# Two warm-up runs of TensorE resized and the gathers of the second block spread differently over its first two tiles

## The chip, the cores and the metric

The kernel runs on one core of a Trainium2 chip. The metric is the device time of one execution in microseconds, the median of several. Its engines are named as in the profile: PE (TensorE matmul), PEld (TensorE weight load), DVE (VectorE), ACT (ScalarE), POOL (GpSimd), SP (SyncE).

## The reference

The kernel is a recommendation tower. For each of 1024 samples, 39 ids pick one row of 16 numbers each out of 39 tables; then three layers of compressed interaction are applied, and a small three-layer network ends it:

```python
e = jnp.stack([tbl_0[ids[:, 0]], ..., tbl_38[ids[:, 38]]], axis=1)     # 1024 x 39 x 16
x0 = xk = e
for idx, (W, b) in enumerate([(w0, b0), (w1, b1), (w2, b2)]):          # each 128 units
    z = jax.nn.relu(jnp.einsum('bhd,bkd,hks->bsd', x0, xk, W) + b[None, :, None])
    # layers 0 and 1: the first 64 units are the next xk, the other 64 go out; layer 2: all 128 go out
logit = jnp.sum(jnp.concatenate(direct, axis=1), axis=-1)              # 1024 x 256
h = jnp.maximum(jnp.concatenate([logit, dense_ctx], axis=1) @ W_top1 + b_top1, 0.0)
h = jnp.maximum(h @ W_top2 + b_top2, 0.0)
y = h @ W_top3
```

All is in float32. 26 tables have 1000 to 125000 rows and are gathered by indirect DMAs; 13 small ones are gathered like the others, except in the first block.

## The kernel before

**Tiles.** The 1024 samples are 8 blocks of 128. A block's 16 embedding columns are cut into 4 tiles of 4 columns, so a tile is 512 wide (4 columns by 128 samples) and there are 32 tiles. Every engine has its own program and walks over steps -2 to 31; step t does layers 1 and 2 of tile t, layer 0 of tile t+1, and the transposes of tile t+2. Steps -2 and -1 are the start, where layers 1 and 2 are absent.

**A product.** DVE multiplies the layer's input with replicated rows of the embedding (`x_rep`, loaded from DRAM by SP and ACT queues for each tile) into 128x1024 products, ten pairs per layer 1 or 2, four for layer 0. `KINDS` (line 33) says how each pair goes on. "U" goes to PE as it is. For "P" and "V" ACT makes a rounded head of the product (line 701) and POOL ("P", line 583) or DVE ("V", line 904) the rest, product minus head, and PE multiplies heads and rests (line 1040). A P pair therefore passes DVE, ACT, POOL and PE in turn. Layer 1 is "UPVPUPVPVP" (P at pairs 1, 3, 5, 7, 9), layer 2 is "UUVUPUVPVP" (P at pairs 4, 7, 9).

**Gathers.** One block's ids need 39 indirect DMAs of 128 rows each (`gather`, line 566), all issued by POOL between its rests. They land in `gathered`, in order of fields, in four groups of 12, 12, 8 and 7 with a semaphore each. ACT's `spread` (line 713) waits for all four groups and copies `gathered` to `emb` (line 719), from which PE transposes tiles; after the copy `gathered` is free and POOL may take the next block's ids (`copy_indices`, line 562). The first block is gathered at the start: 26 big tables by DMA, 13 small ones by one-hot matmuls on PE (lines 1003 to 1008, called the sums below).

The second block's 39 gathers are dealt out by line 41: `GATHERS_EARLY[0]` of them before step 0 (lines 611 to 613), `GATHERS_EARLY[1]` in step 0 and `GATHERS_EARLY[2]` in step 1 (lines 621 to 623). Inside a step `rests` places them by line 40:

```python
GATHERS_AFTER = {1: (0, 1, 0, 0, 8), 2: (2, 2, 2)}   # after the n-th P rest of layer 1, of layer 2
...
                while layer == 2 and fields:
                    gather(fields.pop(0))             # what is left, after the last rest
```

So nine fields fit into layer 1 of a step (one after pair 3, eight after pair 9); what is beyond goes into layer 2, two after pair 4, two after pair 7, the rest after pair 9. The `spread` of the second block is in ACT's step 1, after the head of layer 2's last pair and ahead of all heads of step 2 (lines 783 and 784). Later blocks use 10, 10, 11 and 8 fields in their four steps (line 42), and are not touched.

**PE's start.** PE spreads the ids of the small tables (line 986), transposes the dense features (line 990), waits for the one-hots, runs `keep_busy(FIRST_WARM_UP)`, waits for the last table terms (line 1002), does the sums, waits for the small rows and for the first three groups of gathers, runs `keep_busy(WARM_UP)`, waits for the weights of layer 0, and transposes the first two tiles (line 1094):

```python
            def keep_busy(count):
                for n in range(count):
                    nc.tensor.matmul(z[1][:], onehots[:, n % 4, :],
                                     onehots[:, 0:N // P, :].rearrange("p c b -> p (c b)"), start=True, stop=True)
```

Nothing reads what these matmuls (line 997, bf16, 512 columns) write. After the transposes come ACT's copies (lines 731, 767), SP's store of the rows (lines 536, 539), the first loads of `x_rep` by SP and ACT (lines 519, 688), layer 0 of tile 0 (lines 1017, 1074), and step 0.

Of the kernel before, what the change touches and what calls it, by code (L numbers as in the profile page):

```python
# [37 lines left out]
WHOLE_SLOTS = 6  # L38
SPLIT_SLOTS = 4
GATHERS_AFTER = {1: (0, 1, 0, 0, 8), 2: (2, 2, 2)}  # L40
GATHERS_EARLY = (20, 10, 9)
GATHERS_OF_TILE = (10, 10, 11, 8)
D2_AFTER = 6
XT_AFTER = 3
# [8 lines left out]
EMB_AFTER = 6  # L53
D0_AFTER = 4
AHEAD = 2
WARM_UP = 34
SMALL_RUNS = ((0, 3), (17, 22), (26, 31))
SMALL = tuple(f for start, stop in SMALL_RUNS for f in range(start, stop))
TABLE_ROWS = 125
TERMS = 3  # L60
IDS_PER_BANK = 4
FIRST_WARM_UP = 12
TABLES_OF_ACT = 4
FILL_UP = 10
GATHER_GROUPS = (12, 12, 8, 7)
# [33 lines left out]
def build_kernel(nc, dense_ctx, ids, tables, W_top1, b_top1, W_top2, b_top2, W_top3,  # L99
# [19 lines left out]
    with ExitStack() as ctx:  # L119
# [262 lines left out]
        def wait_gathers(eng, t, groups):  # L382

            for g in groups:
                first = GATHER_GROUPS[g] - sum(group_of[f] == g for f in SMALL)
                eng.wait_ge(s_gather[g], t.blocks(16 * GATHER_GROUPS[g], 16 * first))
# [174 lines left out]
        def _(pool):  # L561
# [4 lines left out]
            def gather(f):  # L566

                nc.gpsimd.indirect_dma_start(  # L568
                    gathered[:, f, :], None, tables[f],
                    bass.IndirectOffsetOnAxis(ap=idx[:, f:f + 1], axis=0)).then_inc(s_gather[group_of[f]], 16)  # L570
# [40 lines left out]
            early = list(range(FIELDS))  # L611
            for f in early[:GATHERS_EARLY[0]]:
                gather(f)
            del early[:GATHERS_EARLY[0]]
            def body(t):
                if not has_layers12(t):
                    return
                ahead = t.plus(AHEAD)
                k = ahead.first % TPB
                refill = None  # L620
                if t.turn is None and t.first < LOOP0:
                    fields = early[:GATHERS_EARLY[1 + t.first]]
                    del early[:GATHERS_EARLY[1 + t.first]]
                elif t.turn is None and ahead.blocks(1, 1) >= BLOCKS:
                    fields = []
                else:
                    first = sum(GATHERS_OF_TILE[:k])
                    fields = list(range(first, first + GATHERS_OF_TILE[k]))
                    if k == 0:
                        refill = ahead.blocks(1, 1)  # L630
                rests(t, 1, fields, refill)
                rests(t, 2, fields)
# [349 lines left out]
        def _(pe):  # L982
# [11 lines left out]
# [6 lines that stand above are left out]
            pe.wait_ge(s_onehot, len(SMALL))  # L1000
            keep_busy(FIRST_WARM_UP)
            pe.wait_ge(s_low, 1)
# [7 lines left out]
            wait_gathers(pe, Tile(0), range(3))  # L1010
            keep_busy(WARM_UP)
            pe.wait_ge(s_w0, 1)
# [143 lines left out]
```

## Time and profile before

| | us |
|---|---|
| median of 3 runs (lowest, highest) | 1265.41 (1264.4, 1268.2) |
| the profiled execution, its own time | 1277.38 |
| its span, first to last instruction | 1275.6 |
| PE busy (share of the span) | 1234.2 (97%) |
| DVE busy | 1162.4 (91%) |
| POOL busy | 901.5 (71%) |
| ACT busy | 708.0 (56%) |

The span is the table's second time less 1.8 us that lie around it. The profiled execution took 12.0 us more than the median of the runs without a profile. A busy PE is counted from the start of a matmul to its modelled end, so 97% says that there are few gaps, not that the array works at its peak.

### The profile page before, as it was taken

Reading aid. Unit: us, or ns where it says so; the run is one execution under the profiler, and the core shown is the slowest. Engines: PE = TensorE matmul, PEld = TensorE weight load, DVE = VectorE, ACT = ScalarE, POOL = GpSimd, SP = SyncE. Lnnn points to the kernel's source line nnn. Section 1 sums busy time; section 2 is a strip of 40 time slices with the busy share of each in tenths; the row PEclk is TensorE's granted clock in tenths of the full one; section 3 lists DMA queues with packets and bytes.
Section 4 is the critical chain, followed back from the end, with each engine's and each line's share of the span. In section 5 each row is a group of like instructions: output and inputs, shape, how many; then the busy total and the mean of one; then the engine's idle time right before and its main releaser. Section 6 shows DMA issues by size and latency. Waiting matters only on the chain.

```text
span 1275.6 us, 15546 instructions
## 1 busy us (share of the span) xinstructions
PE 1234.2 (97%) x4268; PEld 785.7 (62%) x4268; DVE 1162.4 (91%) x1045; ACT 708.0 (56%) x741; POOL 901.5 (71%) x569
## 2 busy tenths in 40 slices
PE   3779999999999999999999999999999999999999
PEld 2446666666666666666666666666666666666654
DVE  7359999999999999999999999999999999999990
ACT  1236655456655665566655655557555655655542
POOL 7568777776887788787877778786878755555440
PEclk7789999999999999999999999999999999999999
DMA  7299887778988888889888888889888878898500
GB/s 212 60 227 214 188 184 183 193 197 208 223 181 183 189 195 198 197 202 220 203 179 188 191 195 200 201 209 221 180 185 187 197 194 198 198 218 198 132 23 0
DMA packets 135922, 234.42 MB, mean 184 GB/s; under 512 B 16403, under 2 KB 25101, under 8 KB 135787
## 3 DMA queue, kind: packets, MB, share of 16 engines
q1 hardware_dynamic: 84335, 151.67, 51.7%
q10 hardware_dynamic: 41994, 79.99, 24.5%
q0 software_dynamic: 9568, 2.47, 2.0%
q8 instruction: 10, 0.16, 0.1%
q14 instruction: 15, 0.12, 0.0%
HBM read 230.21 MB, written 6.23 MB: 185 GB/s over the span
## 4 chain that ended last, share of the span: by engine, by line
PE 80%; DVE 9%; DMA 4%; issue 4%; another core or an unknown queue 1%; ACT 1%; POOL 0%; ACTq 0%; DVEq 0%; SPq 0%
PE z_odd L1040 32%; PE z_even L1040 30%; PE z_odd L1074 6%; PE z_even L1074 6%; DMA x_rep<-x_rows 4%; DVE whole L871 4%; DVE whole_psum L871 1%; DVE x_rep L811 1%; PE whole_psum L1068 1%; DVE rest L904 1%; PE x_even L1068 1%; PE x_odd L1068 1%; PE x_even L1094 1%; PE x_odd L1094 1%
## 5 line engine op out<-in xcount | busy, mean ns | idle before, releaser
L583 POOL TENSOR_TENSOR rest<-whole,head 128x1024 fp32r<-128x1024 f32 x256 | 611.2, 2398 | 251.4 <-ACT head L701 237.5
L871 DVE TENSOR_TENSOR whole<-x_banks,x_rep 128x1024 f32<-128x1024 f32 x448 | 534.7, 1218 | 40.0 <-ACT x_banks L659 36.8
L701 ACT CAST head<-whole 128x1024 fp32r<-128x1024 f32 x256 | 268.7, 1050 | 155.4 <-DVE whole L871 107.7
L568 POOL DMA_INDIRECT gathered<-in_tbl,idx x299 | 287.6, 962 | 82.2 <-issue 74.6
L701 ACT CAST head<-whole_psum 128x1024 fp32r<-128x1024 f32 x192 | 194.8, 1014 | 137.5 <-DVE whole_psum L871 125.2
L871 DVE TENSOR_TENSOR whole_psum<-x_banks,x_rep 128x1024 f32<-128x1024 f32 x192 | 235.8, 1228 | 6.1 <-DMA x_rep<-x_rows 3.3
L904 DVE TENSOR_TENSOR rest<-whole_psum,head 128x1024 fp32r<-128x1024 f32 x192 | 234.7, 1222 | 0.5 <-ACT head L701 0.5
L1040 PE MATMUL z_odd<-head,w_rest 128*128 128x512 f32 x427 | 196.9, 461 | 1.5 <-POOL rest L583 0.9
L1040 PE MATMUL z_odd<-whole,w_whole 128*128 128x512 f32 x400 | 186.8, 596 | 3.7 <-DVE whole L871 3.7
L1040 PE MATMUL z_even<-head,w_rest 128*128 128x512 f32 x405 | 186.4, 460 | 0.8 <-POOL rest L583 0.7
L1040 PE MATMUL z_odd<-head,w_head 128*128 128x512 f32 x460 | 181.9, 395 | 0.0
L1040 PE MATMUL z_even<-head,w_head 128*128 128x512 f32 x436 | 172.4, 395 | 0.0
L1040 PE MATMUL z_even<-whole,w_whole 128*128 128x512 f32 x368 | 170.5, 592 | 0.0
L1040 PE MATMUL z_odd<-rest,w_head 128*128 128x512 f32 x427 | 168.7, 395 | 0.0
L1040 PE MATMUL z_even<-rest,w_head 128*128 128x512 f32 x405 | 160.0, 395 | 0.0
L1040 PEld LDWEIGHTS z_odd<-whole,w_whole 128*128 128x128 f32 x400 | 76.2, 191 | 74.9 <-issue 64.5
L1074 PE MATMUL z_even<-whole,w0s 117*128 117x512 f32 x238 | 106.8, 598 | 3.9 <-DVE whole L871 3.9
L1040 PEld LDWEIGHTS z_even<-whole,w_whole 128*128 128x128 f32 x368 | 69.7, 189 | 64.0 <-issue 58.2
L1040 PEld LDWEIGHTS z_odd<-head,w_head 128*128 128x128 f32 x460 | 86.6, 188 | 32.2 <-issue 15.2
L1040 PEld LDWEIGHTS z_odd<-head,w_rest 128*128 128x128 f32 x427 | 80.5, 189 | 36.5 <-issue 14.9
L1040 PEld LDWEIGHTS z_even<-head,w_head 128*128 128x128 f32 x436 | 82.1, 188 | 30.6 <-issue 14.4
L1040 PEld LDWEIGHTS z_even<-head,w_rest 128*128 128x128 f32 x405 | 76.5, 189 | 31.8 <-issue 14.1
(117 smaller groups left out, 1007.8 us busy)
## 6 DMA issues: line engine op xcount, KB each, us to landing
x_rep<-x_rows ACTq DMA_DIRECT2D x128, 512.0 KB, 11.6
x_rep<-x_rows SPq DMA_DIRECT2D x128, 512.0 KB, 12.2
x_shift<-x_rows SPq DMA_DIRECT2D x93, 546.0 KB
x_rep<-x_rows ACTq DMA_DIRECT2D x32, 384.0 KB
x_rep<-x_rows SPq DMA_DIRECT2D x32, 384.0 KB
x_rep<-x_rows SPq DMA_DIRECT2D x32, 256.0 KB
gathered<-in_tbl,idx POOLq DMA_INDIRECT x299
x_rows<-xt_and_ctx SPq DMA_DIRECT2D x32, 78.0 KB
```

Source lines behind the costliest of these rows:

```text
L568: nc.gpsimd.indirect_dma_start(gathered[:, f, :], None, tables[f], bass.IndirectOffsetOnAxis(ap=idx[:, f:f + 1], axis=0)).then_inc(s_gathe ...
L583: nc.gpsimd.tensor_tensor(rest[:, split_slot(product)], whole_slot(product), head[:, split_slot(product)].bitcast(F32), ALU.subtract).then ...
L701: nc.scalar.copy(head[:, split_slot(product)], src).then_inc(s_head, 1)
L811: nc.vector.tensor_tensor(onehots[:, before_small[i]:before_small[i + 1], :], ids_bank[i].unsqueeze(1).to_broadcast([TABLE_ROWS, each, P]) ...
L871: nc.vector.tensor_tensor(out[0:rows, 0:width, :], xk[0:rows, :].unsqueeze(1).to_broadcast([rows, width, N]), x0, ALU.mult).then_inc(s_pro ...
L904: nc.vector.tensor_tensor(rest[:, split_slot(product)], whole_psum[:], head[:, split_slot(product)].bitcast(F32), ALU.subtract).then_inc(s ...
L1040: mm = nc.tensor.matmul(zz[:], w, x, start=(j == PE_ORDER[layer][0] and i == 0), stop=(j == PE_ORDER[layer][-1] and i == len(terms) - 1))
L1068: mm = nc.tensor.matmul(out, w, x, start=(i == 0), stop=(i == len(terms) - 1))
L1074: mm = nc.tensor.matmul(z_of(t, 0)[:], w0s[0:ROWS0, i, :], whole_slot((t, 0, j))[0:ROWS0, i - 2 * j, :], start=(i == 0), stop=(i == CHUNKS ...
L1094: mm = nc.tensor.transpose(out[0:ROWS0, i * P:(i + 1) * P], rows, ident[:])
```

## The change

Three constants change: the second run of warm-up matmuls has 10 instead of 34, the first 24 instead of 12, and the 39 gathers of the second block are dealt out as 12, 14 and 13 instead of 20, 10 and 9.

```diff
-GATHERS_EARLY = (20, 10, 9)
+GATHERS_EARLY = (12, 14, 13)
...
-WARM_UP = 34
+WARM_UP = 10
...
-FIRST_WARM_UP = 12
+FIRST_WARM_UP = 24
```

## Rows read from the trace of the kernel before

**Rows 1.** The chain of waits in order of time: start us, us, what.
```profile
390.80 6.01 PE z_even L1074 x14
...
426.96 6.01 PE z_odd L1074 x14
```

**Rows 2.** Timeline of PE, the start: start us, us, engine, line, operation, [idle before <-releaser].
```profile
22.09 4.42 PE L997 MATMUL z_odd<-x_rep 125*128 125x512 bf16 x12
31.23 1.14 PE L1005 MATMUL z_even<-x_rep 125*128 125x48 bf16 x24 [4.71 <-DVE x_rep L828]
...
40.58 2.56 PE L1005 MATMUL z_even<-x_rep 125*128 125x48 bf16 x60 [1.18 <-issue]
...
44.58 8.16 PE L997 MATMUL z_odd<-x_rep 125*128 125x512 bf16 x34 [0.40 <-DVE gathered L838]
52.58 0.88 PE L1094 MATMUL x_even<-ident,emb 128*117 128x128 f32 x4
```

**Rows 3.** Timeline of ACT, the start.
```profile
38.51 1.54 ACT L655 CAST w_head<-whole 128x256 fp32r<-128x256 f32 x3
44.63 1.75 ACT L719 COPY emb<-gathered 128x1872 f32<-128x1872 f32 x1 [4.59 <-DVE gathered L838]
```

**Rows 4.** Stretches: length, busy us of five engines, granted clock, DMA share, GB/s.
```profile
29.00:45.80 16.80, 7.18 (x119) 5.56 (x120) 5.45 (x12) 5.34 (x11) 7.40 (x7) 0.50 0.31 69
46.00:52.60 6.60, 6.60 (x33) 3.07 (x31) 4.31 (x8) 0.39 (x1) 5.06 (x4) 1.00 0.03 4
```

**Rows 5.** Timeline of POOL, ahead of step 0 and in step 0.
```profile
72.67 0.94 POOL L568 DMA_INDIRECT gathered<-in_tbl,idx  x1 [0.30 <-issue]
82.61 4.73 POOL L583 TENSOR_TENSOR rest<-whole,head 128x1024 fp32r<-128x1024 f32 x2 [9.00 <-ACT head L701]
...
106.46 2.40 POOL L583 TENSOR_TENSOR rest<-whole,head 128x1024 fp32r<-128x1024 f32 x1
109.02 0.96 POOL L568 DMA_INDIRECT gathered<-in_tbl,idx  x1 [0.16 <-issue]
...
114.48 2.42 POOL L583 TENSOR_TENSOR rest<-whole,head 128x1024 fp32r<-128x1024 f32 x1 [1.18 <-ACT head L701]
```

**Rows 6.** Timeline of PE: last pair of step 0, first P pair of step 2.
```profile
117.81 0.39 PE L1040 MATMUL z_odd<-head,w_rest 128*128 128x512 f32 x1
...
157.47 0.48 PE L1040 MATMUL z_odd<-head,w_rest 128*128 128x512 f32 x1
```

**Rows 7.** Timeline of POOL, step 1.
```profile
141.42 0.94 POOL L568 DMA_INDIRECT gathered<-in_tbl,idx  x1 [0.30 <-issue]
142.55 2.39 POOL L583 TENSOR_TENSOR rest<-whole,head 128x1024 fp32r<-128x1024 f32 x1 [0.18 <-issue]
147.07 2.38 POOL L583 TENSOR_TENSOR rest<-whole,head 128x1024 fp32r<-128x1024 f32 x1 [2.14 <-ACT head L701]
```

**Rows 8.** Timeline of ACT, end of step 1 and first head of step 2.
```profile
150.47 1.75 ACT L719 COPY emb<-gathered 128x1872 f32<-128x1872 f32 x1
153.05 1.05 ACT L701 CAST head<-whole 128x1024 fp32r<-128x1024 f32 x1 [0.82 <-DVE whole L871]
```

**Rows 9.** Queue of the gathers, packets in 37.2-39.5, 146-148, 186-192 us: packets, MB, share.
```profile
q0 software_dynamic: 64, 0.02, 7.7%
...
q0 software_dynamic: 26, 0.01, 2.8%
...
q0 software_dynamic: 64, 0.02, 2.1%
```

**Rows 10.** Timeline of POOL: the gathers beside those packets.
```profile
37.29 0.94 POOL L568 DMA_INDIRECT gathered<-in_tbl,idx  x1 [0.30 <-issue]
...
181.32 0.96 POOL L568 DMA_INDIRECT gathered<-in_tbl,idx  x1
182.59 0.94 POOL L568 DMA_INDIRECT gathered<-in_tbl,idx  x1 [0.30 <-issue]
```

**Rows 11.** Waits of DVE, 190 to 310 us: us in total, times, longest.
```profile
DVE whole L871 <- DMA x_rep<-x_rows: 2.8, 2, 1.8
```

## The prediction, made before the changed kernel ran

> **What bounds the kernel now.** I read the chain of waits first. From about 85 us to the end it is nearly all PE, and in the steady part a step takes 426.96 - 390.80 = 36.16 us [rows 1], with hardly a gap in PE. Nothing that the change touches runs there: it touches only what lies before step 2. So whatever is gained or lost before about 170 us is carried to the end one to one, and two stages have to be priced. The timeline of PE at the start shows the first. The sums run until 44.2, the second warm-up run starts at 44.58, has 34 matmuls in 8.16 us, and the first transpose follows at 52.58 with no idle time noted before it [rows 2]. The transposes need `emb`, whose copy ended at 44.63 + 1.75 = 46.4 [rows 3]. So here the warm-up itself is what the transposes wait for, and with them the stores, the loads of `x_rep` and step 0. The other stage is the hand-over to the second block's gathers in steps 0 and 1: POOL's timeline [rows 5, 7], when PE is due for what POOL makes [rows 6], and ACT's copy of the second block [rows 8].
>
> **The change, part by part.**
>
> *First warm-up, 12 to 24.* The 12 took 4.42 us from 22.09 and ended at 26.5; the sums began only at 31.23, after 4.71 us idle [rows 2]. Twelve more at the same mean of 0.37 us end at 30.9. They fit: cost nothing, covered by DVE's table terms with 0.3 us to spare. If the clock were high all the way they end earlier. Can they gain? The clock was 0.50 from 29.0 to 45.8 [rows 4], but the sums are short, weight-load-bound matmuls (60 in 2.56 us) and what stretched them was idle time "issue" (1.18 us before the one at 40.58), not the clock [rows 2]. The bound for a gain is their faster part, some 1 us; I take 0.
>
> *Second warm-up, 34 to 10.* 24 fewer. The mean over the run is 8.16 / 34 = 0.24 us, but its beginning ran at half clock and the removed ones are the last, at full clock: 33 in 6.60 us from 46.0 on, 0.20 us [rows 4]. Between them, 24 x 0.22 = 5.2 us (bounds 4.8 and 5.8). The run then ends at 47.4, still 1.0 us behind `emb` at 46.4, so all of it is gain on this path: **-5.2 us**.
>
> TensorE ran 1.4 us of the run at the low level (1.2 GHz) and the rest at the high one (2.4 GHz) [rows 2, 4]. The ten reach past 46.0 as well, and the transposes follow at once. The Trainium skill ("TensorE: Matmul & The Clock Gate", the part on the HAM clock gate) says that sustained activity raises the clock and idling takes it back; that would speak against shortening a warm-up only if a gap followed it, and no row shows one here.
>
> *Gathers ahead of step 0, 20 to 12.* POOL's last one started at 72.67, and its first rest at 82.61 came after 9.00 us of waiting for ACT [rows 5]. Eight fewer free POOL 8 x (0.94 + 0.30) = 10 us earlier. With everything 5.2 us earlier, 20 would have fitted too (the wait would still be near 3.8 us). So: 0. The eight moved instructions and their DMAs pay in steps 0 and 1 instead.
>
> *Step 0, 10 to 14 gathers.* Layer 1 takes nine in both. In layer 2 there was one after pair 4's rest; now there are two, two and one. Pair 4's rest ends at 106.46 + 2.40 = 108.86. Two gathers at 1.26 us spacing end at 111.2; pair 7's rest ends at 113.65; two more gathers end at 116.0; so pair 9's rest starts at 116.0, not 114.48 [rows 5], and ends at 118.4. PE is due for it at 117.81 [rows 6]: **+0.6 us**. The last gather and step 1's first rest end at 121.9, when PE (due at 157.47 - 36.16 = 121.3, and 0.6 late) comes for it: no more.
>
> *Step 1, 9 to 13 gathers.* Nine fit into layer 1; the last was issued at 141.42 [rows 7]. Now four follow in layer 2: after pair 4's rest (142.55 + 2.39 = 144.9) at 145.1 and 146.4, pair 7's rest then runs from 147.3 to 149.7, and the last two are issued at 149.9 and **151.1**. But ACT's copy of the block ran at 150.47, in program order ahead of all of step 2's heads [rows 8]. Behind the wait are queued: the copy (1.75 us), the first head of step 2 (1.05, was at 153.05), and with it the loads of `x_rep` that ACT issues; then POOL's rest of pair 1 (2.40), then PE, due at 157.47; PE's transposes of tile 4 wait for the copy too. So PE is late by 151.1 + landing + 1.75 + 1.05 + 2.40 + 0.1 - 157.5 = landing - 1.1 us.
>
> How long is a landing? The shortest in the trace: issued at 37.29, and both gathers' 64 packets through before 39.5, under 2.2 us, with the DMA engines otherwise idle [rows 9, 10]. Under the loads of `x_rep`: the one issued at 141.42 still had 26 packets between 146 and 148, so 4.6 to 6.6 us; two issued at 181.32 and 182.59, which is the same place of their step as the new ones at 145.1 and 146.4, moved 64 packets in 186 to 192, so up to 9.4 us [rows 9, 10]. The new last gather stands behind three others of layer 2 while that load lasts, and I take 7 us, between the two loaded cases: PE late by **+5.9 us** (bounds 1.1 and 8.3).
>
> The Trainium skill ("DMA: Bandwidth & Descriptors", "Anatomy of one DMA — SWDGE (gpsimd) path") gives a DMA from GpSimd a fixed 2.0 us or so plus its bytes. The idle case agrees with it; the loaded ones do not. By it the step-1 wait would be an estimated 1 us and the whole change a gain; that is the first rival below.
>
> *Clock behind that stall.* PE would stand for most of 6 us. After its idle stretches at the start the clock read 0.50, and the second warm-up needed the time from 44.58 to about 46.0 to get it back [rows 2, 4]. At half speed 1.4 us of matmuls lose 0.7 us, the bounds being 0 and 1.7: **+0.8 us**.
>
> *Relief.* From 190 to 310 us DVE waited 2.8 us for `x_rep` in one group [rows 11]. A pause in step 2 lets the loads catch up once; but the same wait is made anew in each step, by a load that follows DVE's own progress. I take 0, bound -2.8.
>
> **Sum:** -5.2 + 0.6 + 5.9 + 0.8 = +2.1 us, against the profiled execution's 1277.4: 1279.5. That execution is 12.0 us above the median of the runs shown, so part of its stretches are not those of an ordinary run. Moved to the median: 1265.4 + 2.1 = **1267.5 us**. The gain at the start is real and is paid back by one wait in step 1. A measurement of this kernel can tell about 0.3%, 3.8 us, from no change; so this forecast is "no change that can be told".
>
> **Rivals.**
>
> *The last gathers land soon (faster).* If they land in about 2.2 us, as at 37.29, the wait costs 1.1 and no clock: -5.2 + 0.6 + 1.1 = -3.5, with the relief of DVE's waits up to -6.3: 1259.1 to 1261.9. For it: ACT's next two loads stand behind its wait and so don't add to the queue. Against it: both loaded cases of the trace [rows 9, 10].
>
> *The start gains little and the wait stays (slower).* In the profiled execution the sums were stretched by idle time before single matmuls until 40.58 [rows 2]. In a run where they aren't, they end some 7 us earlier, the 34 warm-ups start near 37 and end near 45, while ACT's copy can't start before its own casts end at 38.51 + 1.54 = 40.1 and so ends at 41.8 [rows 3]. The warm-up then outlasts `emb` by about 3 us and that is all there is to gain: -2.8 + 0.6 + 5.9 + 0.8 = +4.5, 1269.9; with a landing of 9.4 us and the larger clock cost +7.8, 1273.2. It decides from a landing of 6.3 us on, where the sum passes +3.8. For it: the 12.0 us between the profiled execution and the median.
>
> *The change doesn't do what it says.* The first warm-up delays the sums: only if its twelve new matmuls take over 4.7 us, and then by less than 1 us; or ACT isn't the one that waits for the gathers in step 1: line 715 names all four groups, so it is.
>
> **How the numbers follow.** The forecast, +2.1, has a chance of 0.5; its own range is -1 to +5 (landing 4.6 to 9.4 with the other terms as taken), and of it 0.4 lies within 0.3% and 0.1 above. The early landing has 0.25: 0.2 faster by over 0.3%, 0.05 within. The small gain at the start has 0.25: 0.2 slower, 0.05 within. That makes faster 0.2, same 0.5, slower 0.3. Eight times in ten: from the early landing with half of the relief, 1260.5, to the small gain with a long landing, 1272.5.
>
> **What would show it.** Right: transposes about 5 us earlier, with 10 matmuls on line 997 ahead of them; the first rest of POOL with a wait over 9 us before it; in step 1 the last two gathers between two rests of layer 2, then an idle time of 5 to 9 us on ACT before the second copy on line 719, released by a DMA of `gathered`, and a gap of 5 to 6 us on PE at the start of step 2, with a granted clock under 1 behind it; steps of 36.16 us after that. Wrong: that copy with an idle time under 2 us before it; transposes that move by less than 3 us; or a step 0 whose first rest moves by less than the transposes did.

## The result, and the profile after

The change is slower: 1277.1 us (median of 5 runs, 1275.1 to 1281.1) against 1266.3 us (5 runs, 1264.4 to 1268.2) for the kernel before beside it, a ratio of 1.0087 [1.0068, 1.0106]. A second measurement, in another set, gave 1277.4 against 1268.0, 1.0070 [1.0046, 1.0093]. So it costs 9 to 11 us; the forecast was no change that can be told, 1267.5.

| | kernel before | with the change |
|---|---|---|
| median, first set | 1266.3 us | 1277.1 us |
| profiled execution, its span | 1277.4, 1275.6 | 1275.1, 1273.3 |
| first transposes | 52.58 [rows 2] | 42.71 |
| wait of POOL before its first rest | 9.00 [rows 5] | 15.48 |
| wait of ACT before the second `emb` copy | none [rows 8] | 8.15 |
| layer 0's first matmul in step 0 | 97.9 | 89.5 |
| from there to the same in steps 1, 2 and 3 | 36.16, 36.16, 36.16 | 36.98, 44.40, 36.16 |

The two profiled spans stand the wrong way round: the changed kernel's is shorter by 2.3 us, while its median is longer by 11. The profiled execution of the kernel before was no ordinary one, as its 12 us above the median had said. The sections below therefore compare with a second profile of the unchanged kernel, whose span was 1268.4.

PE at the start, with the change (timeline: start us, us, engine, line, operation, [idle before <-releaser]), against [rows 2]:

```profile
22.01 6.18 PE L997 MATMUL z_odd<-x_rep 125*128 125x512 bf16 x24 [0.20 <-DVE x_rep L811]
30.74 3.62 PE L1005 MATMUL z_even<-x_rep 125*128 125x48 bf16 x90 [2.55 <-DVE x_rep L828]
35.53 2.33 PE L997 MATMUL z_odd<-x_rep 125*128 125x512 bf16 x10 [0.51 <-DVE gathered L838]
42.71 1.18 PE L1094 MATMUL x_even<-ident,emb 128*117 128x128 f32 x4 [4.84 <-ACT emb L719]
```

The 24 end 2.55 us before the sums can start: they fit. The sums are over in 4 us, not 13, and the ten matmuls after them are followed by 4.84 us in which PE waits for ACT's copy. The same stage on ACT and POOL, against [rows 3] and [rows 5]:

```profile
38.91 1.54 ACT L655 CAST w_head<-whole 128x256 fp32r<-128x256 f32 x3
40.81 1.75 ACT L719 COPY emb<-gathered 128x1872 f32<-128x1872 f32 x1 [0.36 <-DMA gathered<-in_tbl,idx]
```

```profile
74.21 4.75 POOL L583 TENSOR_TENSOR rest<-whole,head 128x1024 fp32r<-128x1024 f32 x2 [15.48 <-ACT head L701]
```

Step 1 is where the time went. POOL, with the four gathers of layer 2, against [rows 7]:

```profile
137.48 0.97 POOL L568 DMA_INDIRECT gathered<-in_tbl,idx  x1
138.75 0.94 POOL L568 DMA_INDIRECT gathered<-in_tbl,idx  x1 [0.30 <-issue]
139.72 2.39 POOL L583 TENSOR_TENSOR rest<-whole,head 128x1024 fp32r<-128x1024 f32 x1
142.27 0.96 POOL L568 DMA_INDIRECT gathered<-in_tbl,idx  x1 [0.16 <-issue]
143.53 0.94 POOL L568 DMA_INDIRECT gathered<-in_tbl,idx  x1 [0.30 <-issue]
144.50 2.40 POOL L583 TENSOR_TENSOR rest<-whole,head 128x1024 fp32r<-128x1024 f32 x1
153.91 7.04 POOL L583 TENSOR_TENSOR rest<-whole,head 128x1024 fp32r<-128x1024 f32 x3 [7.00 <-ACT head L701]
```

ACT, against [rows 8]:

```profile
141.93 1.05 ACT L701 CAST head<-whole 128x1024 fp32r<-128x1024 f32 x1
151.13 1.75 ACT L719 COPY emb<-gathered 128x1872 f32<-128x1872 f32 x1 [8.15 <-DMA gathered<-in_tbl,idx]
152.79 1.04 ACT L701 CAST head<-whole 128x1024 fp32r<-128x1024 f32 x1
```

And PE, against [rows 6]:

```profile
148.22 1.88 PE L1040 MATMUL z_odd<-whole,w_whole 128*128 128x512 f32 x4
153.01 1.19 PE L1094 MATMUL x_even<-ident,emb 128*117 128x128 f32 x4 [2.91 <-ACT emb L719]
156.31 0.80 PE L1040 MATMUL z_odd<-head,w_rest 128*128 128x512 f32 x1 [2.11 <-POOL rest L583]
```

The reader follows one wait down three engines: the last gather is issued at 143.53, ACT stands from 142.98 to 151.13, POOL stands 7.00 us behind ACT's head, and PE waits twice, 2.91 and 2.11 us. The stretches (length, busy us of PE, PEld, DVE, ACT and POOL, granted clock, DMA share, GB/s) show what comes after each gap of PE:

```profile
41.00:45.80 4.80, 3.09 (x10) 2.35 (x11) 4.12 (x7) 3.10 (x4) 2.60 (x3) 0.50 0.07 18
52.60:68.00 15.40, 15.40 (x18) 4.92 (x17) 2.48 (x3) 0.00 (x0) 4.73 (x5) 0.50 1.06 261
153.40:160.20 6.80, 4.69 (x13) 3.61 (x13) 4.62 (x4) 4.67 (x6) 6.29 (x3) 0.50 1.07 206
160.20:171.00 10.80, 10.80 (x44) 8.05 (x44) 9.92 (x9) 4.16 (x5) 6.95 (x6) 1.00 0.27 56
```

### The profile page after: what moved, and what is told of

The parts are those of the page before. It is cut to its first block, busy times and chain, and to the rows that moved or that the text cites. A ratio compares the mean times of both kernels' runs of the same rounds, so it can differ in the third digit from the quotient of the medians.

```text
span 1273.3 us, 15522 instructions
## 1 busy us (share of the span) xinstructions
PE 1235.9 (97%) x4256; PEld 784.2 (62%) x4256; DVE 1164.8 (91%) x1045; ACT 707.6 (56%) x741; POOL 902.3 (71%) x569
## 4 chain that ended last, share of the span: by engine, by line
PE 80%; POOL 7%; DVE 5%; issue 4%; DMA 3%; ACT 1%; DVEq 0%; POOLq 0%; ACTq 0%
PE z_odd L1040 31%; PE z_even L1040 30%; PE z_even L1074 7%; PE z_odd L1074 6%; POOL gathered L568 4%; POOL rest L583 3%; DVE whole L871 3%; DMA x_rep<-x_rows 2%; DVE whole_psum L871 1%; PE whole_psum L1068 1%; DVE rest L904 1%; PE x_odd L1094 1%; PE x_odd L1068 1%; PE x_even L1094 1%; PE x_even L1068 1%
## 5 line engine op out<-in xcount | busy, mean ns | idle before, releaser
L871 DVE TENSOR_TENSOR whole<-x_banks,x_rep 128x1024 f32<-128x1024 f32 x448 | 534.0, 1216 | 35.3 <-ACT x_banks L659 33.5
L871 DVE TENSOR_TENSOR whole_psum<-x_banks,x_rep 128x1024 f32<-128x1024 f32 x192 | 235.5, 1226 | 6.4 <-DMA x_rep<-x_rows 4.2
L1074 PE MATMUL z_even<-whole,w0s 117*128 117x512 f32 x238 | 110.7, 617 | 0.0
```

Source lines behind the costliest of these rows:

```text
L871: nc.vector.tensor_tensor(out[0:rows, 0:width, :], xk[0:rows, :].unsqueeze(1).to_broadcast([rows, width, N]), x0, ALU.mult).then_inc(s_pro ...
L1074: mm = nc.tensor.matmul(z_of(t, 0)[:], w0s[0:ROWS0, i, :], whole_slot((t, 0, j))[0:ROWS0, i - 2 * j, :], start=(i == 0), stop=(i == CHUNKS ...
```

## The experiments

Eleven runs were made, in three sets, each set beside its own runs of the kernel before; one of the eleven is the kernel before itself and one the changed kernel again. "Steps" are the distances between the first matmuls of layer 0 (line 1074) in one step and the next, from step 0 to 1, 1 to 2 and so on; the wait for the gathers falls into the second.

**The kernel before once more.** No edit. It asks how far one profile can be trusted.

> The kernel before once more, unchanged, for a second profile of it. Theory A (the first profile was not an ordinary execution: its sums were stretched by idle time of PE, and DVE and ACT were held up 5 us each ahead of step 0): ratio 1.00, the sums done by about 36 us, the 34 warm-up matmuls from about 36 to 45 us, transposes near 45, and the first rest of POOL some 10 us or more before 82.6. Theory B (the start of the first profile is the ordinary one and the 12 us of difference lie elsewhere): transposes at 52 to 53 us again.

Measured: 1268.45 us, ratio 0.9997 [0.9982, 1.0012], span 1268.4. PE at the start:

```profile
31.98 3.51 PE L1005 MATMUL z_even<-x_rep 125*128 125x48 bf16 x90 [5.48 <-DVE x_rep L828]
36.65 7.51 PE L997 MATMUL z_odd<-x_rep 125*128 125x512 bf16 x34 [0.51 <-DVE gathered L838]
44.00 0.87 PE L1094 MATMUL x_even<-ident,emb 128*117 128x128 f32 x4
```

The sums take 4 us without a gap, where [rows 2] shows them from 31.23 to 44.2, with idle "issue" of 1.18 us before the matmul at 40.58; there were seven such gaps, of 0.45 to 1.23 us. The warm-up ends at 44.16, and ACT's copy of `emb` (41.06 + 1.75 here) at 42.81. So in this execution the second warm-up outlasts `emb` by 1.35 us, not by 6.4, and little more can be gained there by shortening it. DVE's timeline shows a further wait, 40 us later:

```profile
87.72 4.08 DVE L871 TENSOR_TENSOR whole<-x_odd,x_shift 117x1024 f32<-117x1024 f32 x4 [2.82 <-DMA x_shift<-x_rows]
```

**The change taken apart.** The gathers alone, and the second warm-up alone, and both warm-ups:

```diff
-GATHERS_EARLY = (20, 10, 9)
+GATHERS_EARLY = (12, 14, 13)
```

> Only the gathers are dealt out as 12, 14 and 13; both warm-up runs as before. Theory A (two separate losses, of which the wait of ACT for the last gathers in step 1 is one): slower by 7 to 9 us, 1.0055 to 1.007, step 1 to step 2 about 44 us instead of 36.16, ACT idle some 8 us ahead of its second copy on line 719. Rival C (the clock at the start is the whole loss, and the wait in step 1 would be absorbed in a run whose start is ordinary): within 2 us of before. Rival D (all of the loss is the gathers): slower by 11 us.

```diff
-WARM_UP = 34
+WARM_UP = 10
```

> Only the second warm-up run is shortened, 34 to 10. Theory A (TensorE idles from the end of the ten until emb is there, its clock falls to the low level and layer 0 ahead of step 0 runs at half speed for most of 20 us): slower by 3 to 5 us, 1.0025 to 1.004, granted clock 0.50 for ten us or more between 40 and 67 us. My recorded reasoning (the warm-up is what the transposes wait for, so shortening it is a gain): faster by 3 to 5 us. Rival D: no change.

```diff
-WARM_UP = 34
+WARM_UP = 10
-FIRST_WARM_UP = 12
+FIRST_WARM_UP = 24
```

> Both warm-up runs as in the change (24 and 10), gathers 20, 10 and 9 as before: the change without its gathers. Theory A: change less this one is the price of the gathers, 7 to 9 us, so slower than before by 2 to 4 us. If the twelve added matmuls of the first run keep the clock up they would take back part of what second_run_10 loses; I expect within 1.5 us of second_run_10. Rival C: slower by 11 us.

Measured: gathers alone 1276.5 us, 1.0054 [1.0030, 1.0078]; second run 1268.4, 0.9999 [0.9984, 1.0014]; both runs 1269.1, 1.0005 [0.9992, 1.0019]. The gathers make the loss and the warm-ups make nothing that can be told. Theory A of the shorter second run was right on the clock and wrong on the time: the granted clock did read 0.50 behind the transposes, and the loss of 3 to 5 us did not come (stretch of the second run alone):

```profile
42.00:54.00 12.00, 12.00 (x20) 5.08 (x20) 5.14 (x6) 1.54 (x3) 9.29 (x10) 0.50 0.62 139
```

That the gathers make the loss shows in the first two steps too: 39.30 and 44.93 with the gathers alone, 37.89 and 36.15 with the second run alone, 37.86 and 36.15 in the kernel before. With the gathers alone ACT's copy again stands:

```profile
152.03 1.75 ACT L719 COPY emb<-gathered 128x1872 f32<-128x1872 f32 x1 [8.02 <-DMA gathered<-in_tbl,idx]
```

With the second run alone, the 24 matmuls gone from PE come back at once as a wait for `emb`, and then DVE waits longer for the first load of layer 0's rows (timelines of PE and DVE):

```profile
35.68 2.33 PE L997 MATMUL z_odd<-x_rep 125*128 125x512 bf16 x10 [0.51 <-DVE gathered L838]
41.81 1.18 PE L1094 MATMUL x_even<-ident,emb 128*117 128x128 f32 x4 [3.80 <-ACT emb L719]
```

```profile
87.61 4.08 DVE L871 TENSOR_TENSOR whole<-x_odd,x_shift 117x1024 f32<-117x1024 f32 x4 [8.55 <-DMA x_shift<-x_rows]
```

The transposes start 2.2 us earlier than in the kernel before, and this instruction starts at 87.61 instead of 87.72. The chains of waits of the two kernels name the load (start us, us, what); first the kernel before, then the second run alone:

```profile
64.65 22.99 DMA x_shift<-x_rows
```

```profile
61.20 26.33 DMA x_shift<-x_rows
```

Issued 3.45 us earlier, it took 3.34 us longer. These two profiles differ in the clock as well: it read 0.50 from 48.6 to 69.1 us in the first and from about 41 to 55 us in the second. That such a load lands at the same time whenever it is issued does not follow from them. In the five profiles in which the clock read 0.50 for 3.4 us or less between the transposes and this load, the load was issued anywhere from 58.79 to 66.29 and landed 25.0 to 25.4 us later in all five.

**Which step's gathers.** Step 1 with 13 and step 0 as it was (ahead of the tiles 20, then 6, to keep the sum); step 0 with 14 and step 1 as it was; and one gather in layer 2 of step 1:

```diff
-GATHERS_EARLY = (20, 10, 9)
+GATHERS_EARLY = (20, 6, 13)
```

> Gathers 20, 6 and 13: step 1 loaded as in the change, the early stretch as before, step 0 lighter than before. Theory A (the price is ACT's wait in step 1, for two gathers behind pair 7 of layer 2): slower by 6 to 9 us, 1.005 to 1.007; the step that holds the copy on line 719 about 44 us. Rival E (the price is that POOL is overloaded, by 14 gathers in step 0 and 13 in step 1 together): slower by at most 3 us.

```diff
-GATHERS_EARLY = (20, 10, 9)
+GATHERS_EARLY = (16, 14, 9)
```

> Gathers 16, 14 and 9: step 0 loaded as in the change, step 1 as before. Theory A: the recorded 0.6 us and no more, 1.000 to 1.001; ACT's second copy on line 719 without an idle time before it. Rival E: slower by 3 us or more.

```diff
-GATHERS_EARLY = (20, 10, 9)
+GATHERS_EARLY = (20, 9, 10)
```

> Gathers 20, 9 and 10: one single gather of step 1 falls into layer 2, behind the rest of pair 4, about 5 us before ACT comes to the copy. With landings of 5 to 9 us under load ACT would wait 1 to 4 us for it, and PE, which has 0.9 us in hand there, 0 to 3 us: 1.000 to 1.002. If landings were near 2.2 us there: no wait on ACT and 1.000. If what counts is only that a gather stands in layer 2 at all: the full 7 us.

Measured: step 1 alone 1276.4 us, 1.0054 [1.0034, 1.0073]; step 0 alone 1268.8, 0.9995 [0.9978, 1.0011]; one in layer 2 1269.2, 1.0004 [0.9985, 1.0023]. Thirteen gathers in step 1 alone lose as much as the gathers of the change together (1.0054 both). There ACT waited 8.05 us before the copy, and the step from 1 to 2 took 44.80. Step 0's four more cost nothing that can be told. The single gather of layer 2 stands between the two (its timelines of POOL and ACT):

```profile
136.71 0.97 POOL L568 DMA_INDIRECT gathered<-in_tbl,idx  x1 [0.16 <-issue]
```

```profile
145.64 1.76 ACT L719 COPY emb<-gathered 128x1872 f32<-128x1872 f32 x1 [3.58 <-DVE whole_psum L871]
```

The view names DVE as releaser, whose product had just ended; but line 719 reads `gathered`, not a product. The gathers' queue still moved packets between 144 and 145 us, 9 of them (DMA view of that stretch), and none from 145.0 to 145.6:

```profile
q0 software_dynamic: 9, 0.00, 1.8%
```

So here too the gather is the likely releaser, issued 8.9 us before the copy. The step took 38.06 us, 1.9 more than 36.16, which a ratio of 1.0004 with an interval of 0.4% in all cannot show.

**More warm-up instead of less.** If PE's start carried to the end, 24 more matmuls would cost some 5 us.

```diff
-WARM_UP = 34
+WARM_UP = 58
```

> The second warm-up run with 58 matmuls instead of 34, gathers as before: transposes about 5.2 us later (24 times 0.215). Theory F (DVE's first layer 0 of step 0 waits for the load of x_shift, and the loads since the first store fill the DMA engines, so the end of that wait follows the store): the loads start later too, so slower by 3 to 5 us, 1.0025 to 1.004. Rival G (what ends that wait does not follow the transposes, as it seems between 34 and 10): within 1 us.

Measured: 1272.9 us, 1.0022 [1.0005, 1.0039], 2.8 us (0.6 to 4.9). The transposes came at 48.22, 4.2 us later, and DVE's first layer 0 waited 8.13 us for `x_shift`, whose load was issued at 66.29 and took 25.38. So later does cost, here 2.8 of the 4.2 us. Theory F's range began at 3, and its sign and size are near; why earlier gained nothing with ten matmuls is not answered by it.

**Can the load be brought forward?** A theory was that 1 MB of `x_rep` that ACT asks for in step 0 delays the `x_shift` load, and that the shorter warm-up would pay with those loads placed later.

```diff
-heads(t, 1, start=n, upto=n + 1, loads={1: [0], 2: [1]} if has_layer0(t) else {})
+heads(t, 1, start=n, upto=n + 1, loads={8: [0], 9: [1]} if is_first(t) else
+      {1: [0], 2: [1]} if has_layer0(t) else {})
```

> The kernel before, but in step 0 ACT issues its two early loads of x_rep (for tile 1, 1 MB) with the heads of pairs 8 and 9, not 1 and 2. Theory F (the load of x_shift that DVE waits for ahead of its layer 0 of step 0 shares full DMA engines with whatever else is under way, so its end is set by volume): at some 200 GB/s, 1 MB less ahead of it is up to 5 us; x_shift lands 2 to 5 us earlier and the kernel gets faster by 1 to 4 us, 0.997 to 0.999. Rival G (the load ends near 87 for another reason): lands at 87 again, ratio 1.000, or slower, if tile 1 then waits for its rows.

The same with the second warm-up at 22:

> The same with a second warm-up run of 22 matmuls instead of 34, which ends about where emb is there, so that transposes come 1 to 1.5 us earlier and the clock stays up over them. Theory F: with the DMA engines still full from the first store to x_shift's landing, that second gain is only partly passed on: within 1 us of loads_later. If it were passed on in full: 1 to 1.5 us faster than loads_later.

Measured: 1272.8 us, 1.0030 [1.0013, 1.0047], and 1272.6 us, 1.0035 [1.0020, 1.0049]. The theory's gain failed (timeline of DVE, the first kernel; its lines from here on stand one higher, so L872 is L871 of before):

```profile
87.97 4.08 DVE L872 TENSOR_TENSOR whole<-x_odd,x_shift 117x1024 f32<-117x1024 f32 x4 [3.65 <-DMA x_shift<-x_rows]
116.15 1.23 DVE L872 TENSOR_TENSOR whole<-x_banks,x_rep 128x1024 f32<-128x1024 f32 x1 [4.64 <-DMA x_rep<-x_rows]
```

The load of `x_shift` landed at 87.9 as before, after 23.83 us, and the rows of the next tile came 4.64 us late. With 22 matmuls the load was issued at 58.79 and landed at 84.0, after 25.20 us, so it did move; but DVE still waited 4.3 us for the next tile's `x_rep`, and in step 0 PE waited 7.5 us at once for POOL, whose first rest followed directly on the last of its 20 gathers. Most of the 5.3 us by which the load was issued earlier (64.06 and 58.79) is the clock and not the transposes, which moved by 1.1: with 34 matmuls it read 0.50 from about 48 to 68 us, with 22 it stayed at 1.00 until 66. Nor is that profile a typical one, for its mean granted clock was 0.988 and that of the other eleven executions 0.980 to 0.985. Both kernels lose more than they gain.

**The change once more**, in that last set:

> The changed kernel once more, beside its parts' siblings. If its loss is that of its gathers alone (gathers_alone 1.0054, step1_alone 1.0054, both warm-up runs together 1.0005), it reads 1.005 to 1.007 here. If the parts add up to more than their sum, as its first reading of 1.0087 would have it, 1.008 or more.

Measured: 1277.4 us, 1.0070 [1.0046, 1.0093]; steps 37.66 and 44.23; ACT's wait 8.36 us. No kernel here beats the one before.

## Why the prediction was wrong

**The base and the second warm-up (the step that failed).** "24 fewer ... -5.2" was worked out from where `emb` stood against the end of the warm-up in one profiled execution, and the sums of that execution had been stretched by some 9 us (12.9 instead of 4.2). The signs were in front of me: "issue" gaps before single matmuls, and 12 us above the median. I used them for a rival and not for the sum; moving the sum's result to the median does not repair a term that exists only in the stretched execution. In ordinary ones the transposes start at 43.4 to 44.4 with 34 matmuls and at 41.8 to 42.7 with ten, so 1.7 us earlier in the mean, and even this brought nothing: ratio 0.9999 for the second run alone, 1.0005 for both. Term: predicted -5.2, measured 0, with +0.05% [-0.08, +0.19] for the pair. The prediction's own sign of being wrong, transposes that move by less than 3 us, came.

**A gap behind the shortened warm-up.** This is the second thing that the step had wrong. The prediction set the clock rule aside because no row showed a gap there. With ordinary sums there is one, 4.84 us, and the granted clock reads 0.50 (1.2 GHz) in the stretches from 41.00 to 68.00. That agrees with what the Trainium skill ("TensorE: Matmul & The Clock Gate", the part on the HAM clock gate) says of idling. The nine ordinary profiles whose warm-up is 34 or 10 and whose loads are as before show where the 1.7 us went:

| second warm-up, profiles | clock at 0.50 between the transposes and the end of layer 0 ahead of step 0 | from the transposes to layer 0 in step 0 |
|---|---|---|
| 34: gathers alone, step 0 alone, one in layer 2 | at most 3.4 us | 43.8, 43.2, 43.5 us |
| 34: kernel before again, step 1 alone | about 20 us | 46.1, 46.1 us |
| 10: second run alone, both runs | about 13 us | 47.1, 47.2 us |
| 10: the change, twice | about 25 us | 46.8, 46.8 us |

All four profiles with ten matmuls lost the clock, and of the five with 34 two did for long; the stretch is 2.3 to 4.0 us longer where it was lost. Where it was kept, an earlier start did carry as far as layer 0 in step 0: transposes at 42.3, 43.9, 44.1, 44.4 and 48.2 us, with 22, 34, 34, 34 and 58 matmuls, and layer 0 at 85.4, 87.1, 87.6, 88.2 and 93.0. The executions without a profile fit: the mean granted clock was 0.978 to 0.985 in the twelve of the second run alone and 0.982 to 0.989 in the thirty of the kernel before beside them, on average 0.9825 and 0.9868. The difference, 0.0043 of 1268 us at half clock, is by my estimate some 11 us more at the low level. In the profiles of the change and of step 1 alone the chain of waits runs through layer 0 ahead of step 0 on PE at half clock, and DVE, which comes late itself, hardly waits for `x_shift` (the change):

```profile
86.57 4.08 DVE L871 TENSOR_TENSOR whole<-x_odd,x_shift 117x1024 f32<-117x1024 f32 x4 [0.77 <-DMA x_shift<-x_rows]
```

In the second run alone and in both runs the clock was back by 56 us; there PE first waited 2.96 and 2.84 us for POOL, whose first rest stood directly behind the last of its 20 gathers, and then DVE 8.6 and 8.7 us for `x_shift`. So three things stand on this stretch that the prediction had at nothing: the clock, POOL's gathers and a load. That the clock is what the shorter warm-up costs is the account that these rows favour, and it isn't shown: no run holds the clock up and leaves the rest as it is.

**First warm-up.** Predicted 0: right. The 24 end 2.55 us before the sums start; both runs and the second run alone differ by 0.06%.

**Step 0.** Predicted +0.6. With step 0's gathers alone the ratio is 0.9995 [0.9978, 1.0011]. The first step took 36.98, 37.66, 38.31 and 39.30 us in the four profiles with 14 gathers in step 0, and 37.86, 37.89 and 38.05 in the three ordinary ones with 10. No cost is seen, and one of 0.6 isn't excluded.

**Step 1, the mechanism.** Right in each of its links: the copy on line 719 waits, then ACT's head, POOL's rest, PE. I took a landing of 7 us; it was 151.13 - 143.53 = 7.6. In the same execution the last gather of the start was issued at 38.29, with a DMA share of 0.10, and the chain of waits gives it 2.34 us. Right also was that the fixed 2.0 us or so of the Trainium skill ("DMA: Bandwidth & Descriptors", "Anatomy of one DMA — SWDGE (gpsimd) path") doesn't hold here: with the engines full, the gathers took 7.6 us and, with one in layer 2, some 8.9. The stretch before the copy, in the changed kernel, with a DMA share of 1.05:

```profile
140.00:153.40 13.40, 10.06 (x36) 6.32 (x35) 8.73 (x8) 4.95 (x5) 6.42 (x4) 1.00 1.05 244
```

**Step 1, the size.** Predicted 5.9 + 0.8 = 6.7 us; the step took 44.40 - 36.16 = 8.2. PE's timeline in the second profile of the kernel before:

```profile
148.99 1.88 PE L1040 MATMUL z_odd<-whole,w_whole 128*128 128x512 f32 x4
150.71 0.87 PE L1094 MATMUL x_even<-ident,emb 128*117 128x128 f32 x4
151.33 0.48 PE L1040 MATMUL z_odd<-head,w_rest 128*128 128x512 f32 x1
```

Beside it, with the change: from the last group of step 1 to the transposes 4.79 us instead of 1.72, so 3.1; from these to the first P matmul 3.30 instead of 0.62, so 2.7; a wait of 0.44 for a rest of layer 2, which the two gathers before it made late, and which I had not counted. That is 6.2, against 5.9. The clock is the rest: the 18 matmuls of heads and rests from 156.31 on took 6.09 us to the next group, 4.30 at full clock (as in the kernel with one gather in layer 2), so 1.8. It had read 0.50 from 153.40 to 160.20, not for the 1.4 us that I took from the second warm-up. The term for the clock was 0.8 with an upper bound of 1.7, and measured 1.8.

**The sum.** 0 + 0 + 8.2 and at most +0.6 make 8 to 9 us, where the two measurements say 8.9 and 11.0 with intervals of 2.4 to 3.0 us to either side. Measured apart, the gathers give 0.54% [0.30, 0.78], 6.8 us, and the warm-ups 0.05%. That the whole costs a little more than its parts lies within the intervals, and stays unsettled. Of the rivals, "the start gains little and the wait stays" came nearest, and its reason, sums that aren't stretched, was right. Its 1269.9 was low: it still took 2.8 us as gained at the start, without the clock, and had the step-1 wait at 6.7 and not 8.2. It had a chance of 0.25 and should have had the first place.

## What to carry to other kernels

Before a term is taken from a profiled execution, compare its time with the median: 12 us above it meant that one stage was stretched, and every "what ends last" read in that stage was false. Before something is shortened at a start, ask what the next instruction will wait for instead, and whether TensorE stands still meanwhile and goes on at the low clock; then follow the path down to the first steady step, and look for an instruction there that already waits for a DMA or for another engine. And a transfer moved later on an engine of its own is a wait for whoever reads its tile in program order: here one that stood in front of heads, rests and matmuls.

## What the hardware showed unexpectedly

The clock at the start isn't the same from one execution to another, even with the same warm-up of 34. The second profile of the kernel before, with its transposes straight behind the warm-up, read:

```profile
41.00:48.60 7.60, 7.60 (x30) 4.29 (x29) 5.52 (x10) 3.35 (x5) 4.54 (x5) 1.00 0.07 19
48.60:69.10 20.50, 20.50 (x25) 6.80 (x24) 3.46 (x4) 0.65 (x1) 15.62 (x17) 0.50 1.00 262
```

The kernel with the gathers alone, whose start is the same, read:

```profile
50.20:53.60 3.40, 3.40 (x5) 1.13 (x4) 0.84 (x1) 0.00 (x0) 2.49 (x3) 0.53 0.99 253
53.60:60.00 6.40, 6.40 (x15) 2.29 (x14) 1.91 (x2) 0.00 (x0) 4.88 (x6) 1.00 1.06 262
```

PE had no gap ahead of either fall. The first lost clock for 20.5 us and the second for 3.4, and layer 0 in step 0 still started at 90.1 and 88.2: DVE's wait for `x_shift` was 2.82 in the one and 7.78 in the other and took up most of the difference. What makes the clock fall in one execution and not in the other is not shown here. Why that load lands where it does stays open too. In the nine profiles whose chain of waits names it, it was issued between 58.8 and 66.3 and took 23.0 to 26.3 us, while the DMA share stood at about 1: 25.0 to 25.4 in the five with the clock high, 23.0 and 23.8 in two of 34 matmuls with the clock low, 26.3 twice with ten. Placing 1 MB of ACT's loads later changed nothing with 34 matmuls. That it is the backlog of the engines fits these rows, and isn't shown.
